# Taylor attention of a four-layer block on one Trainium2 core: values instead of kernels of scores as TensorE's stationary operand

## The reference, cut to what matters

```python
def taylor_exp(x):                       # 1, x/2, and all products x_i x_j / (4 sqrt 2)
    x2 = (x[..., :, None] * x[..., None, :]).reshape(*x.shape[:-1], FD * FD) / R2
    return jnp.concatenate([jnp.ones_like(x[..., :1]), x / RRD, x2 / RD], axis=-1)
k_enc_f, q_f, k_f = taylor_exp(k_enc), taylor_exp(q), taylor_exp(k)
A_qk = jnp.tril(jnp.einsum('bhnd,bhmd->bhnm', q_f, k_f))
y1 = jnp.einsum('bhnm,bhme->bhne', A_qk, v)
A_qk2 = jnp.einsum('bhnd,bhmd->bhnm', q_f, k_enc_f)
y2 = jnp.einsum('bhnm,bhme->bhne', A_qk2, v_enc)
k_state = k_enc_f.sum(axis=2, keepdims=True) + jnp.cumsum(k_f, axis=2)
z = 1.0 / ((q_f * k_state).sum(axis=-1) + EPS)
out = (y1 + y2) * z[..., None]
return out.transpose(0, 2, 1, 3).reshape(b, n, H * HD) @ Wout.T
```

## Time and profile before

| | us |
|---|---|
| median of 3 executions (1793.17, 1793.24, 1802.02) | 1793.24 |
| the profiled execution, its own time | 1782.04 |
| its span, first to last instruction | 1780.2 |
| first scores of this stage to the last add of its output | 761.19 to 1048.43 |

### The profile page before, as it was taken

The page is one execution under the profiler, slowest core; times in us unless marked ns, Lnnn a source line. Parts: engine busy times, 40 slices in busy tenths (PEclk is TensorE's granted clock), DMA queues, the critical chain, the costliest instruction groups (busy, mean ns, idle before and its releaser), DMA issues. The chain is left out here.

```text
span 1780.2 us, 31999 instructions
## 1 busy us (share of the span) xinstructions
PE 1575.2 (88%) x10960; PEld 1094.2 (61%) x10960; DVE 1183.5 (66%) x3106; ACT 1002.4 (56%) x2683; POOL 375.5 (21%) x386
## 2 busy tenths in 40 slices
PE   4799999959999999899999989588989957899986
PEld 2577777726666666567778766355556733555653
DVE  5599998747777777646545434577743358999964
ACT  2488887706666666444454434133453427888845
POOL 0100000000000000010122015332452410888830
PEclk8899999979999999989999999799999978999998
DMA  4000000040000000110000011400012130233200
GB/s 141 1 1 1 1 1 1 1 141 1 1 1 1 1 1 1 55 57 1 13 16 16 25 31 64 165 1 1 15 36 62 46 90 14 88 86 89 86 21 24
DMA packets 43980, 62.50 MB, mean 35 GB/s; under 512 B 7576, under 2 KB 29920, under 8 KB 43008
## 3 DMA queue, kind: packets, MB, share of 16 engines
q1 hardware_dynamic: 39280, 51.08, 9.6%
q0 software_dynamic: 4544, 9.38, 1.5%
HBM read 49.88 MB, written 15.75 MB: 37 GB/s over the span
## 5 line engine op out<-in xcount | busy, mean ns | idle before, releaser
L591 ACT ACTIVATE probs<-psum_all,pair_negmax 128x256 f32<-128x256 f32 x512 | 235.8, 473 | 158.9 <-DVE pair_negmax L690 86.7
L2116 POOL TENSOR_TENSOR weighted<-state,c_all 128x512 f32<-128x512 f32 x128 | 163.6, 1298 | 77.5 <-DVE state L2126 62.5
L690 DVE TENSOR_REDUCE pair_negmax<-psum_all 128x2 f32<-128x512 f32 x192 | 123.6, 685 | 66.9 <-PE psum_all L506 66.9
L2126 DVE TENSOR_TENSOR_SCAN state<-decay,psum_all 128x512 f32<-128x512 f32 x128 | 148.9, 1199 | 15.4 <-PE psum_all L2044 12.5
L716 DVE TENSOR_SCALAR probs<-probs,pair_recip 128x256 f32<-128x256 f32 x512 | 146.1, 349 | 4.5
L506 PE MATMUL psum_all<-keys,queryT 64*128 64x256 f32 x1024 | 143.9, 400 | 2.8 <-ACT probs L591 2.7
L602 ACT ACTIVATE probsT<-psum_all 128x512 f32<-128x512 f32 x256 | 140.0, 611 | 0.7 <-PE psum_all L517 0.5
L531 PE MATMUL psum_all<-probsT,values 128*64 128x256 f32 x1024 | 138.8, 392 | 0.0
L517 PE MATMUL psum_all<-ident,probs 128*128 128x128 f32 x1024 | 133.1, 273 | 2.8 <-ACT probsT L602 1.9
L517 PEld LDWEIGHTS psum_all<-ident,probs 128*128 128x128 f32 x1024 | 119.1, 141 | 18.1 <-issue 4.4
L506 PEld LDWEIGHTS psum_all<-keys,queryT 64*128 64x128 f32 x1024 | 92.6, 189 | 54.6 <-issue 46.6
(11 more groups left out here) (369 smaller groups left out, 3281.4 us busy)
## 6 DMA issues: line engine op xcount, KB each, us to landing
c_all<-c_rows SPq DMA_DIRECT2D x64, 256.0 KB, 3.3
slots<-slot_fill_dram SPq DMA_DIRECT2D x2, 2535.0 KB, 14.6
ring<-slots SPq DMA_DIRECT2D x18, 260.0 KB, 3.0
keys<-found SPq DMA_DIRECT2D x16, 256.0 KB, 4.7
up<-up_dram SPq DMA_DIRECT2D x1, 2048.0 KB, 7.8
down<-down_dram SPq DMA_DIRECT2D x1, 2048.0 KB, 12.3
up<-up_dram SPq DMA_DIRECT2D x1, 1408.0 KB, 6.1
found<-values,dest POOLq DMA_INDIRECT x78, 2.2
```

Source lines behind the costliest of these rows:

```text
L591: nc.scalar.activation(k.probs[:, 2 * (u % PAIR_BUF) + j, t, :], k.psum[score_bank(u, j)][:, SEQ * t:SEQ * (t + 1)], ACT.Exp, bias=k.pair_ ...
L690: nc.vector.reduce_max(k.pair_negmax[:, u % 2, SUB * j:SUB * (j + 1)], src, AXX, negate=True).then_inc(s.negmax_ready, 1)
L2116: nc.gpsimd.tensor_tensor(w.weighted[:, u % RING, :], w.state[:, u % RING, :], w.c_all[:, u // L3_DC % C_RING, :], ALU.mult)\
L2126: nc.vector.tensor_tensor_scan(w.state[:, u % RING, :], w.decay[:, u % L3_RING, :, :].rearrange("p b n -> p (b n)"), k.psum[u % PARTS_RING ...
```

## The change

The values become the stationary operand and the kernels of scores stream past them. For each half of 32 of the 64 value columns, the four heads of a quad each fill 32 columns of the array and write 32 partitions of the result, which so has head and value on partitions and queries along the row: the layout that `outT` needs. `y_turn`, `y`, `product` and the ScalarE copies 1534 and 1517 go. The denominators come from a third such product in which 32 columns of ones are stationary, so each arrives repeated over its head's 32 partitions; VectorE inverts 256 of them per partition (`invert`) and multiplies straight out of PSUM into `outT` (`normalise`). The product needs two banks (5 and 6), so the encoded scores of four heads share bank 4; two of them are now made ahead of the other scores and two behind them, with a wait between. `output` moves by two steps, into kind D (for the last sequence, to step 33). The rows of the output weights are permuted on the host. Cut to its core:

```diff
@@ taylor_jobs @@
-        for n in range(QUADS):
-            slots[2][QUADS * q + n + 2].append(("y_turn", q, n))
-        slots[0][QUADS * q + 6].insert(0, ("output", q, 0))
+        slots[0][QUADS * q + (8 if q + 1 < BATCH else 5)].insert(0, ("output", q, 0))
@@ taylor_attention_stage @@
-    EB, OB, JB = 4, 6, 7
+    EB, AB, DB, JB = 4, 5, 6, 7
+    HALF = HD // 2
+    enc_scores = k.psum[EB].rearrange("p (c n) -> p c n", c=2)
...
-                        wait_saved(pe, ("y_turn", q, QUADS - 1))
+                        pe.wait_ge(s.normed, QUADS * (q + 1))
@@ TensorE, scores @@
+                    def encoded_scores(j):
+                        return nc.tensor.matmul(enc_scores[L1_ENC * (j % 2):L1_ENC * (j % 2 + 1), j // 2, :], w.k_encT[rows_of(j), q % 2, n // 2, :],
+                                                w.query[rows_of(j), q % 2, n, :], start=True, stop=True)
+
+                    encoded_scores(0)
+                    encoded_scores(1).then_inc(s.enc_started, 1)
+                    for keys, queries in ((slice(0, P), slice(0, SEQ)), (slice(P, 2 * P), slice(P, SEQ))):
+                        for j in (2, 3, 0, 1):
+                            nc.tensor.matmul(k.psum[j][:, keys.start // P * SEQ:][:, 0:queries.stop - queries.start], w.kT[rows_of(j), q % 2, n // 2, keys],
+                                             w.query[rows_of(j), q % 2, n, queries], start=True, stop=True)
+                    pe.wait_ge(s.enc_started, g + 1)
+                    encoded_scores(2)
+                    last = encoded_scores(3)
+                    last.then_inc(s.scores_ready, 1)
+
+                def add_up(g, into, of_enc, of_keys, first, last_part):
+
                     for j in range(4):
+                        nc.tensor.matmul(into[rows_of(j), :], of_enc(j), w.kernel_enc[:, g % 2, j // 2, :], start=first, stop=False)
+                    for kt, keys, queries in ((0, slice(0, SEQ), slice(0, SEQ)), (1, slice(SEQ, WIDE), slice(P, SEQ))):
+                        for j in range(4):
+                            last = nc.tensor.matmul(into[rows_of(j), queries], of_keys(j, kt), kernel_of(g, j)[:, keys], start=False, stop=(last_part and kt == 1))
+                    return last
+
+                def weigh_ones(g):
...
+                    pe.wait_ge(s.kernel_ready, 3 * (g + 1))
+                    if g >= 1:
+                        pe.wait_ge(s.norm_ready, g)
+                    add_up(g, k.psum[DB][:, 0:SEQ], lambda j: w.ones[:, 1 + j % 2, :], lambda j, kt: w.ones[:, 0, :], True, True).then_inc(s.weighed, 1)
+
+                def weigh_values(g):
...
+                    if g >= 1:
+                        pe.wait_ge(s.normed, g)
+                    for half in range(2):
+                        cols = slice(HALF * half, HALF * (half + 1))
+                        last = add_up(g, k.psum[AB][:, SEQ * half:SEQ * (half + 1)], lambda j: w.v_enc[:, q % 2, 2 * n + j // 2, j % 2, cols],
+                                      lambda j, kt: w.values1[:, q % 2, kt, 8 * (n // 2) + 2 * j + n % 2, cols], half == 0, half == 1)
                     last.then_inc(s.weighed, 1)
@@ TensorE, in step g @@
-                        weigh(g - 1, 0)
+                        weigh_ones(g - 1)
                     for job in slots[1][g]:
                         do(job)
                     if 0 <= g - 1 < N:
-                        weigh(g - 1, 1)
+                        weigh_values(g - 1)
@@ ScalarE @@
-                    nc.scalar.activation(w.kernel_enc[:, g % 2, :, :], k.banks[:, EB:EB + 2, 0:SEQ], ACT.Square, scale=0.25, bias=1.0).then_inc(s.squared, 1)
-
-                def save_product(g, c):
...
+                    nc.scalar.activation(w.kernel_enc[:, g % 2, :, :], enc_scores, ACT.Square, scale=0.25, bias=1.0).then_inc(s.squared, 1)
@@ VectorE @@
-                def normalise(g, c):
...
+                def invert(g):
+                    dve.wait_ge(s.weighed, 2 * g + 1)
+                    nc.vector.tensor_scalar(w.norm[:, g % 2, :], k.psum[DB][:, 0:SEQ], 2 * L1_EPS, None, ALU.add).then_inc(s.norm_ready, 1)
+                    dve.wait_ge(s.norm_ready, g + 1)
+                    nc.vector.reciprocal(w.recip[:, g % 2, :], w.norm[:, g % 2, :]).then_inc(s.recip_ready, 1)
+
+                def normalise(g):
+                    q, n = g // QUADS, g % QUADS
+                    dve.wait_ge(s.weighed, 2 * (g + 1))
+                    if q >= 2 and n == 0:
+                        wait_made(dve, ("output", q - 2, 0))
+                    dve.wait_ge(s.recip_ready, g + 1)
+                    nc.vector.tensor_tensor(k.outT[:, q % 2, 2 * n:2 * n + 2, :], k.psum[AB][:, :].rearrange("p (a n) -> p a n", a=2),
+                                            w.recip[:, g % 2, :].unsqueeze(1).to_broadcast([P, 2, SEQ]), ALU.mult).then_inc(s.normed, 1)
...
-                        normalise(g - 1, 0)
+                        invert(g - 1)
...
-                        normalise(g - 1, 1)
+                        normalise(g - 1)
```

More of the change, by code:

```diff
@@ L1347, in job_bank @@
     def job_bank(job):
-        return k.psum[OB if number[job] < filling and (filling - number[job]) % 2 == 0 else JB]
+        return k.psum[DB if number[job] < filling and (filling - number[job]) % 2 == 0 else JB]
     def by_act(job):
-        return job[0] in ("values", "enc_values", "y_turn")
+        return job[0] in ("values", "enc_values")
     def saved_count(job):
@@ L1376, in _ @@
                 low, high = slice(0, L1_ENC), slice(L1_ENC, P)
[L1377 to L1382, removed]
+                for n, (part, value) in enumerate(((w.ones[:, 0, :], 1.0), (w.ones[low, 1, :], 1.0), (w.ones[high, 1, :], 0.0), (w.ones[low, 2, :], 0.0),
+                                                   (w.ones[high, 2, :], 1.0), (w.v_enc[low, :, :, 1, :], 0.0), (w.v_enc[high, :, :, 0, :], 0.0))):
+                    if n:
+                        pool.wait_ge(s.background, n)
+                    nc.gpsimd.memset(part, value).then_inc(s.background, 1)
+                pool.wait_ge(s.background, 7)
                 nc.gpsimd.memset(k.gate_cmp[:, :, :, :], 0.0).then_inc(s.cleared, 1)
@@ L1444, in scores @@
                         pe.wait_ge(s.squared, 3 * g)
-                    for j in range(4):
[L1446 to L1457, removed]
+                    def encoded_scores(j):
+                        return nc.tensor.matmul(enc_scores[L1_ENC * (j % 2):L1_ENC * (j % 2 + 1), j // 2, :], w.k_encT[rows_of(j), q % 2, n // 2, :],
+                                                w.query[rows_of(j), q % 2, n, :], start=True, stop=True)
@@ L1463, in weigh @@
+                def weigh_values(g):
+                    q, n = g // QUADS, g % QUADS
+                    if n == 0:
                         wait_saved(pe, ("enc_values", q, 0))
                         wait_saved(pe, ("values", q, 3))
[L1465 to L1477, removed]
+                    if g >= 1:
+                        pe.wait_ge(s.normed, g)
@@ L1540, in _ @@
                         square(g)
-                    for c, slot in enumerate(slots):
+                    for slot in slots:
                         for job in slot[g]:
                             do(job)
-                        if c < 2 and 0 <= g - 1 < N:
-                            save_product(g - 1, c)
                     if g == TAYLOR_GATE.exp:
@@ L2633, in lay_out @@
     by_pair = [8 * half + 4 * c + 2 * j + one for half in range(2) for one in range(2) for c in range(2) for j in range(2)]
-    a["w_out1"] = rows_first(i["L1_attn_Wout"].T.reshape(HEADS, HD, P)[by_pair].reshape(HEADS * HD, P), PAIRS)
+    of_quad = [[8 * (n // 2) + 2 * j + n % 2 for j in range(4)] for n in range(QUADS)]
+    a["w_out1"] = rows_first(i["L1_attn_Wout"].T.reshape(HEADS, 2, HD // 2, P)[of_quad].transpose(0, 2, 1, 3, 4).reshape(HEADS * HD, P), PAIRS)
     a["w_v_enc1"] = a["w_v_enc1"].reshape(P, HEADS, HD)[:, by_pair[0::2] + by_pair[1::2]].reshape(P, HEADS * HD)
```

46 lines of the change are left out of this document (9 added, 37 removed).

## The result

The changed kernel took 1805.64 us, the median of 8 executions (1804.31 to 1809.22), against 1793.20 for the kernel before beside it (8 executions, 1789.81 to 1802.02). The ratio is 1.0071, with a 95% interval from 1.0056 to 1.0086: slower by 12.4 us, where 8.2 were forecast. The profiled execution took 1809.22 around a span of 1807.1, against 1780.2. That is 26.9 more, over twice the difference of the medians, so the spans as a whole can't be compared and I read the stage alone. From its first to its last matmul it took 303.0 us, and 292.1 before: 10.9 more.

What follows compares the result with a forecast made beforehand. TensorE's order of work was taken to bound the stage. First four steps +2.3, steps 4 to 27 +9.6 and the end -3.7 gave +8.2 us, a median of 1801.4, range 1784 to 1813.

Steps and rivals of the forecast that it cites:

- kind D: Step of the round A, B, C, D that now carries `output`, with `query_keys` and `enc_keys`: forecast 11.89 us.
- The split scores: TensorE's scores in each step: the separate encoded pair costs its full group, 0.57 us, so 1.46 becomes 2.03.
- The wait for ScalarE's copy: TensorE ahead of the slot-1 job: stays 2.74 us behind the scores in A, 3.35 in C, swallowing the ones' saving.
- C: Third step of a round: slot-1 job stays 3.35 us behind the scores; forecast 8.70 us.
- A and B: First two steps of a round: scores, wait, job and values sum to 8.09 us each.
- The last steps: From step 28 on: VectorE's chain bounds steps 29 and 30 at 5.9 us each; whole stretch 39.3, so -3.7.
- first four steps: 4 x 0.57 = +2.3: Start of the stage: only the split scores' 0.57 us a step is added, +2.3 us.
- Steps 4 to 27: Six rounds, each 2.34 us longer, +14.0, less one `output` of 4.44: +9.6 us.
- Rival 1: First encoded pair hides beside the other heads' scores: -9.0 us, 1784.2; chance 0.2.
- Rival 2: VectorE's reciprocal is slower, making ones wait past 3.0 us; at 3.6, +21 us, 1814; chance 0.12.
- Rival 3: The four heads' products run one behind another on TensorE: some 300 us more; chance 0.01.
- Rival 4: The kept TensorE waits are shorter and it goes on at once: 16 us below the forecast, 1785; chance 0.07.

Runs made afterwards that it cites:

- run 2: The kernel before with only its scores split, two encoded heads ahead of the other scores and two behind: 1814.17 us, ratio 1.0093.
- run 3: The kernel before with split scores, encoded weights loaded 128 columns wide so all scores have shape 32*128, part of the encoded scores left out: 1794.78 us, ratio 1.0002.
- run 7: The changed kernel with encoded scores of four heads in one group again and values and ones both ahead of the slot-1 job: 1771.94 us, ratio 0.9961.
- Run 6: The changed kernel with the products of ones and values one behind the other, both ahead of the slot-1 job: 1796.95 us, ratio 1.0000.
- run 4: The changed kernel with each reciprocal made twice, the first into a spare buffer: 1816.97 us, ratio 1.0119.
- run 5: The changed kernel with the reciprocal replaced by a plain copy, leaving out the inversion of the denominators: 1789.79 us, ratio 1.0066.
- run 8: The changed kernel again, unchanged, profiled beside other executions of the kernel before: 1794.53 us, 15.4 above the kernel before of its set.
- run 1: The kernel before, unchanged, profiled once more: 1792.34 us.

## Why the prediction was right, and where it was off

**Direction and order of size** were right: +12.4 against +8.2, inside the range.

**The split scores** were put at 0.57 a step: 2.03 us for the scores, 2.02 measured. The row pointed that way: the weights of the second shape are loaded only when the matmuls of the first are out. By the Trainium skill (TensorEngine Tiling (Array Packing), Key Properties) changing the tiling mode drains TensorE, and runs 2 and 3 agree: 0.55 a step with the change of shape, nothing without. The other page of the Trainium skill (TensorE: Matmul & The Clock Gate, Part 3), by which matmuls on different row groups overlap, is not contradicted: in run 3 they start 0.02 us apart with one shape, and in run 2, with two, they do not overlap.

**Products and waits.** Forecast were 1.21 for the ones and 2.29 for the values. The values took 2.30, and the ones 1.20 where a job follows them at once (run 7, 774.63 to 775.83). The wait for ScalarE's copy was kept as it stood: the second job came 2.75 behind the scores in A (2.74) and 3.33 in C (3.35). So A and B took 8.10 (8.09), C 8.68 (8.70), D 11.82 (11.89). Run 6 shows that this wait is where the products' saving went.

**VectorE.** The reciprocal of 1.8 us, from the slope between 4 and 16 elements, took 1.75. The last steps took 5.63 (5.9), and the last output kept its pace (3.81 for 3.7), so the end gave back 4.4 rather than 3.7.

**The mis-sized term** is the first of the sum, "first four steps: 4 x 0.57 = +2.3". It measured +4.6: +3.9 in the first two steps, +0.7 in the third and next to nothing in the fourth. The working added 0.57 a step and took the clock to be as before. The window of the first 24.6 us of the stage, before and after:

```profile
755.84:780.46 24.62, 21.97 (x114) 13.67 (x114) 7.82 (x19) 8.95 (x15) 5.28 (x8) 0.78 0.27 102
```
```profile
758.29:782.91 24.62, 22.68 (x94) 11.26 (x98) 6.18 (x14) 8.16 (x13) 5.38 (x10) 0.64 0.27 102
```

The granted clock is 0.64 instead of 0.78 and TensorE gets through 94 records instead of 114. The same window, from 5.35 us ahead of the first scores on, has 0.64 in all six profiles with a change of shape ahead of their scores (after, and runs 2, 4, 5, 6 and 8), and 0.78, 0.81, 0.86 and 0.86 in the four without (before, and runs 1, 3 and 7). The first two steps took 23.4 to 26.0 us in the six and 18.3 to 19.7 in the four; runs 2 and 3, nearly the same program, have 26.0 and 18.3. In the 30 us from the first scores on the clock was at the lower of its two levels (1.2 and 2.4 GHz) for 13.1 us in the changed kernel and for 5.6 in the kernel before. Half of the difference, about 3.7 us, is an estimate of what that cost; it covers the 2.8 that the first two steps took above their 2 x 0.57. So the loss comes with the change of shape, but how the split keeps the clock at the lower level for longer was not found.

**Steps 4 to 27** came to +10.6 for +9.6, but with the 2.69 us of step 14 in it; without that it is 1.7 below the forecast, mostly since step 8 of the kernel before, 9.2 us for 7.23, was itself longer than its kind, by more than the 0.64 in the changed kernel. It holds the gate's job `counts` (run 7), which the working had in neither. **Luck:** without step 14's excess the three stretches sum to +8.2, the forecast to a tenth, but only because +2.3 in the first four steps cancels -1.7 in the next and -0.7 at the end. **Left over** of the median's +12.4 are 1.4 to 4.4 us: the stage without the odd step is 8 to 11 us longer (300.3 and 300.1 against 292.1 and 289.3). The other stages differ from execution to execution by more than that, and I can't place it.

**The rivals.** Rival 1 (the pair hides) is refuted by run 2, and run 3 says why. Rival 2 (the reciprocal) by runs 4 and 5: neither doubling it nor taking it away moves a round. Its point of decision, 3.0 us, was too low: at 3.45 the rounds held. Rival 3 (the heads one behind another) by the row of the ones, 16 further records in 0.83 us. Rival 4 (the waits vanish) by the 1.03 us that end with ScalarE's 1518, and by run 6.

**Slips of the working,** none of which moves the forecast: 879.18 is the start of the second job's weight load, and its matmul starts at 879.21, so the stretch in A was 2.77 and not 2.74. The forecast's own range, 8.2 less 5.6, begins at +2.6 and not at +1. And by its own steps the chances are 0.13 for faster and 0.52 for same.

## What to carry to other kernels

In these runs work on different rows of the array ran abreast within one tile shape (32*128) and not across two (32*64 and 32*128), so keep all groups of one shape together, or give them one shape: the group split around another shape paid its full length twice. Before counting a shorter product as a gain, ask what its engine was waiting for around it; here the saving of 0.5 us a step lay ahead of a wait for ScalarE and vanished, and moving the product into the wait brought it back. Each wait filled here brought the next one out (VectorE's copies in runs 6 and 7).

## What the runs showed that was not expected

- Step 14 is at times 2 to 7 us longer, in kernels of either kind (after 2.69, run 1 2.2, runs 4 and 6 over 5, run 3 6.9; 0.2 in run 2, nothing in before and in runs 5, 7 and 8). TensorE, VectorE and ScalarE stand still at once while GpSimd sends rows by indirect DMA (in the changed kernel it pauses too, for 2.04 us; in run 4 it goes on), and the profile names no releaser in the core:

```profile
896.04 0.51 PE L1446 MATMUL psum_all<-keys,probsT 32*128 32x128 f32 x4 [0.23 <-issue]
897.59 0.69 DVE L1591 TENSOR_TENSOR outT<-psum_all,recip 128x512 f32<-128x512 f32 x1 [3.17 <-remote]
897.67 0.65 PE L1439 MATMUL psum_all<-keys,k_encT 32*64 32x256 f32 x4 [1.12 <-remote]
```

- A stage that no kernel here changes, the attention of layer 2 with its 1844 matmul records, took 195.4, 207.1, 210.2 and 196.5 us in four profiles (before, run 1, after, run 8), at granted clocks of 0.99, 0.97, 0.95 and 0.99, and 197.0 to 210.2 in the other six. Run 2, the kernel before with its scores split, is among the longest, so it is not the changed kernel that lengthens it. It accounts for 14.8 of the 26.9 us between the spans:

```profile
1144.80:1340.20 195.40, 166.55 (x1844) 104.79 (x1844) 132.22 (x207) 75.35 (x98) 81.68 (x103) 0.99 0.11 38
```
```profile
1158.50:1368.70 210.20, 174.18 (x1844) 108.96 (x1844) 132.13 (x207) 75.32 (x98) 81.66 (x103) 0.95 0.10 35
```
